# First stage of a two-layer attention and expert network: the product of the normalised rows with the attended rows is made by GpSimd instead of VectorE

## The reference, cut to what matters

```
c = layernorm(x)
s = (c @ w_c + b_c) + (q @ w_q + b_q) + einsum(c, q, w_cq) + b_cq
a = softmax(s, over q)          c2q = a @ q
b = softmax(max(s), over c)     q2c = b @ c      (one row for each sequence)
z = concat([c, c2q, c * c2q, c * q2c]) @ W_l.T + b_l
x = x + z
```

## Time and profile before

| what | value |
|---|---|
| time, median of 3 runs | 1287.81 us (1287.68 to 1289.49) |
| span of the profiled execution | 1303.4 us |
| TensorE busy in the span | 1239.4 us (95%) |
| VectorE busy | 998.1 us (77%) |
| ScalarE busy | 813.5 us (62%) |
| GpSimd busy | 512.1 us (39%) |
| mean granted TensorE clock | 0.982 of full speed |

### The profile page before, as it was taken

How to read it: one execution, slowest core, us unless ns; L and a number is a source line. 1 busy time by engine, 2 the same in 40 slices (tenths; PEclk the granted TensorE clock), 3 DMA queues, 4 the chain that set the end, 5 groups by cost and what they waited for, 6 DMA issues and landing times.

```text
span 1303.4 us, 44045 instructions
## 1 busy us (share of the span) xinstructions
PE 1239.4 (95%) x17244; PEld 1117.8 (86%) x17245; DVE 998.1 (77%) x2454; ACT 813.5 (62%) x1552; POOL 512.1 (39%) x553
## 2 busy tenths in 40 slices
PE   6899999984999999998899999999999999999997
PEld 5788888874999999996688888888888888888886
DVE  4888888875555555536988898889888988898884
ACT  4477766642655555565567666766676667666753
POOL 2466666654121212135544344424442444343010
PEclk9899999997899999998899999999999999999999
DMA  3124333112422222213101110111011101110000
GB/s 110 64 80 147 96 122 82 64 68 71 134 82 72 80 72 80 73 53 76 33 16 34 35 33 16 34 34 29 21 35 34 33 16 34 34 33 12 11 11 18
DMA packets 86536, 71.21 MB, mean 55 GB/s; under 512 B 25088, under 2 KB 73216, under 8 KB 86368
## 3 DMA queue, kind: packets, MB, share of 16 engines
q1 hardware_dynamic: 74768, 42.71, 11.4%
q0 software_dynamic: 11600, 26.10, 6.5%
HBM read 40.73 MB, written 28.05 MB: 53 GB/s over the span
## 4 chain that ended last, share of the span: by engine, by line
PE 83%; DVE 10%; issue 3%; POOL 1%; ACT 1%; DMA 1%; another core or an unknown queue 0%; SPq 0%; DVEq 0%; POOLq 0%; ACTq 0%
PE c_ps_w L84 23%; PE d_ps_y L1218 10%; PE c_ps_w L1731 8%; PE d_ps_h L84 8%; PE c_ps_s L1697 5%; PE c_ps_w L1720 4%; PE c_ps_w L1706 4%; PE c_ps_w L1748 4%; PE a_ps_w L84 3%; PE a_ps_w L917 2%; PE a_ps_w L872 2%; PE a_ps_w L825 1%; PE d_ps_x L1197 1%; PE c_ps_w L1603 1%; DVE a_a_diag L670 1%
## 5 line engine op out<-in xcount | busy, mean ns | idle before, releaser
L1484 POOL DMA_INDIRECT c_back<-sorted_y,k_y_row_of x112 | 112.8, 1007 | 177.8 <-PE c_ps_w L1720 144.8
L93 POOL DMA_INDIRECT sorted_x<-a_xn,f_slot_of x128 | 127.9, 999 | 84.5 <-PE a_ps_w L917 36.6
L1218 PE MATMUL d_ps_y<-e_w_all,d_h_t 128*128 x1136 | 139.1, 276 | 0.0
L1083 POOL DMA_DIRECT2D sorted_y<-d_y_rows x71 | 50.8, 716 | 213.0 <-DVE d_y_rows L1114 208.8
L1218 PEld LDWEIGHTS d_ps_y<-e_w_all,d_h_t 128*128 128x128 f32 x1136 | 134.0, 193 | 0.0
L1731 PEld LDWEIGHTS c_ps_w<-c_wo,c_o_t 128*128 128x128 f32 x1024 | 122.5, 192 | 5.6 <-ACT c_o_t L1945 1.4
L1731 PE MATMUL c_ps_w<-c_wo,c_o_t 128*128 128x128 f32 x1024 | 124.9, 275 | 0.9 <-ACT c_o_t L1945 0.6
L1945 ACT COPY c_o_t<-c_ps_w 128x512 f32<-128x512 f32 x128 | 68.8, 590 | 78.4 <-PE c_ps_w L1720 78.4
L1510 POOL TENSOR_TENSOR c_rstd<-c_var,c_minus_half 128x1 f32<-128x1 f32 x64 | 35.7, 558 | 200.0 <-DVE c_var L2135 200.0
L1166 ACT ACTIVATE d_h_t<-d_ps_h,d_biases 128x256 f32<-128x256 f32 x284 | 111.7, 475 | 2.5 <-PE d_ps_h L84 2.1
L2152 DVE TENSOR_TENSOR c_shifted<-c_ps_s,c_mask 128x1024 f32<-128x1024 f32 x64 | 78.0, 1219 | 41.7 <-PE c_ps_s L1697 41.6
(11 more groups left out here) (264 smaller groups left out, 3596.1 us busy)
## 6 DMA issues: line engine op xcount, KB each, us to landing
d_x_rows<-sorted_x SPq DMA_DIRECT2D x71, 128.0 KB, 2.1
sorted_y<-d_y_rows POOLq DMA_DIRECT2D x71, 128.0 KB, 2.2
k_X<-in_x SPq DMA_DIRECT2D x16, 256.0 KB
a_q_rows<-in_ctx SPq DMA_DIRECT2D x16, 256.0 KB
ctx_cols<-a_q_t SPq DMA_DIRECT2D x16, 256.0 KB
k_ctx_raw<-ctx_cols SPq DMA_DIRECT2D x16, 256.0 KB, 3.9
out<-k_X SPq DMA_DIRECT2D x15, 256.0 KB, 3.1
sorted_x<-a_xn,f_slot_of POOLq DMA_INDIRECT x128
```

The costliest lines, as they stand in the source:

```text
L93: pool.indirect_dma_start(out=sorted_x, out_offset=bass.IndirectOffsetOnAxis(ap=slot_of[:, choice, t:t + 1], axis=0), in_=xn2[:, k, :], in ...
L1218: last = pe.matmul(ps_y[c % 2][:, k * D:(k + 1) * D], h_t[c % 2][:, j, k * P:(k + 1) * P], w2_all[:, ds(e * HC + j, 1), :].rearrange("p a ...
L1484: pool.indirect_dma_start(out=back[:, choice, k, :], out_offset=None, in_=sorted_y, in_offset=bass.IndirectOffsetOnAxis(ap=y_row_of[:, cho ...
```

## The change

GpSimd gets a new step, `cross`, as the last of its turn, behind `root1`: it waits until `z` of the group before has been made (the last reader of `cc_t`) and until `c2q_t` of its own group is complete, and then makes the same product of the same two buffers into the same third. VectorE's instruction for it is taken out. The semaphore that `make_z` waits for is the same and is now raised by GpSimd. Nothing else is changed.

```diff
@@ gpsimd
+            def cross(g):
+
+                if g >= 1:
+                    pool.wait_ge(full, full_at("z", g - 1))
+                pool.wait_ge(c2q_ready, NB * (g + 1))
+                pool.tensor_tensor(cc_t[:], c2q_t[:], c_t[g % 2][:], ALU.mult).then_inc(cc_ready, 1)
+
@@ gpsimd, the end of a turn
                 if t + 2 < G:
                     root1(t + 2)
+                if a is not None:
+                    cross(a)
@@ vector, weighted(g)
-                dve.tensor_tensor(cc_t[:], c2q_t[:], c_t[g % 2][:], ALU.mult).then_inc(cc_ready, 1)
```

## The result

The changed kernel takes 1306.29 us (median of 4 runs, 1301.10 to 1307.24); the kernel before took 1288.65 beside it (4 runs). The ratio is 1.0128, 95 % interval [1.0113, 1.0142]: 17.6 us slower. The forecast was 1294.1, with 1298.7 as its upper end: the direction was right, the size too small by more than half.

What follows compares the result with a forecast made beforehand. VectorE's list between L648 and L842 was taken to set the steady turn. 0 for L716, 5.6 for held ranks and 0.7 for the last group, 6.3 in all, added to 1287.81 gave 1294.1 us; range 1288.4 to 1298.7.

Steps and rivals of the forecast that it cites:

- the slack at L648: At the scores' maxima in turns 3 to 14, VectorE waits 0.625 us a turn, which absorbs part of each delay.
- The hold: At L562 and L563, the product begins as L562 ends and holds L563 about 1.09 us; 0.465 a turn remains.
- the price from the earlier trace: At L2176 in the third stage, a GpSimd product cost VectorE's second two-operand instruction about 1.09 us.
- The last group: In turn 16, `z` starts about 0.7 us later behind the product; bounds 0 to 3.0, the upper if TensorE's clock falls.
- L716 is worth nothing: Removing VectorE's product, 0.73 us a turn, gains 0, since the wait for `gate` at L550 grows to 1.34.
- the twelve turns: Products of turns 2 to 13 meet the ranks of turns 3 to 14: 12 x 0.465 = 5.6 us, bounds 0 to 7.9.
- the delay of the first scatters: On GpSimd, the first scatter issues some 1.6 us later, the second about 1; the delay is gone by the third.
- the clock stays up in steady turns: At TensorE in the 12 turns; the rival, a clock falling every turn, gave 34 us, 1322, chance 0.04.
- GpSimd is the one that waits: Rival at the ranks: the product waits until L566, turns cost nothing, the last group 0.7; 1288.5 us, chance 0.15.
- VectorE's relief counts: Rival: the end of VectorE's turn sets the pace, 16 x 0.73 = 11.7 us go, 1276.1 us, chance 0.05.

Runs made afterwards that it cites:

- the second of before: The kernel before, unchanged, profiled once more: 1289.01 us, ratio 0.9995, profile span 1287.8 where the first profile had 1303.4.
- the run with one comparison more: The kernel before with a first rank comparison made twice on VectorE, ahead of L562 in each turn: 1294.99 us, ratio 1.0053.
- the fill: The kernel before, with GpSimd filling a 128 by 1280 tile with zeros at the place of the change: 1288.49 us, ratio 1.0003.
- the half product: The changed kernel with GpSimd making only the first 256 of 512 columns, VectorE the others where L716 was: 1293.57 us, ratio 1.0043.
- idle, 1.03 us: The kernel before, with GpSimd also multiplying a constant tile by itself at the place of the change, result unread: 1299.23 us, ratio 1.0079.
- full, later: The changed kernel with the product of groups 2 to 14 put behind the second scatter of the next turn: 1308.40 us, ratio 1.0153.
- full, earlier: The changed kernel with the product right behind `root2` in the same turn, `root1` behind it, ahead of the last two scatters: 1307.62 us, ratio 1.0150.
- the last kernel: GpSimd's product waits for VectorE's four normalised rows, ahead of its last scatter; VectorE writes 128 by 8 unread zeros where L716 stood: 1288.69 us, ratio 0.9994.

## Why the prediction was right in direction and too small

The first stage is where nearly all of it is lost: the spans of the two profiles, after and the second of before, are 17.7 us apart, and the experts' first matmuls, at 326.1 and 309.6, already 16.5. By the starts of `gate` that is 10.9 in eleven turns, 2.24 in the turn after them, 2.5 in the last group, and 0.9 in the rest.

**The step that failed: the slack at L648.** The prediction took 0.625 off each hold, from the earlier trace rows, and wrote that "the first stage's turns are the same work in both", the profiled execution and the runs. They were the same work but not the same time: that execution had turns of 17.1 where the usual one has 16.73, and in it VectorE had a wait at L648 that the second profile doesn't have and the run with one comparison more rules out for the runs. The 15.6 us between its span and the median was a sign, and it was put aside, though 4.35 of it is all that lies in these turns. What the runs have is 0.2 at L575, behind L648, where the prediction saw nothing idle. With it a turn loses 1.20 - 0.2 = 1.00 instead of 0.465: 12 turns cost 12 us and not 5.6. Of the difference, 12 x 0.425 = 5.1 is the slack and 12 x 0.11 = 1.3 the longer hold. What held L648 back in that one execution stays open: the records of the scores stand where they stand in the other.

**The hold: nearly the right size, in the wrong order.** 1.20 us instead of 1.09, and on the first comparison rather than the second. The prediction had the product wait for the end of L562 and become 1.5 to 1.6 long; it didn't wait, and was 1.26. The sentence on the Trainium skill (SBUF — State Buffer, Who interferes with whom) gave all of the product, 1.28; the measured 1.20 of 1.26 lies by it, so the page was nearer than the price from the earlier trace rows. The same section says that a GpSimd instruction that only writes is no contender, and that a VectorE operation with one tensor and scalars can take the shared ports in a fast mode. The comparison beside the fill (0.42) and the normalisation (1.30 us) agree with both. How the price goes with length and place:

| product | held on VectorE | lost us | turn longer by |
|---|---|---|---|
| half, 0.72 to 0.94 us | second comparison | 0.53 | 0.30 |
| idle, 1.03 us | first comparison | 0.97 | 0.75 |
| full, 1.26 us | first comparison | 1.20 | 1.00 |
| full, later | sum of the counts | 1.50 | 1.22 |
| full, earlier | a row normalisation | 0.96 | 0.90 |

The first four stand ahead of L575 and get 0.2 to 0.3 back there; the last stands behind it and gets 0.06.

**The last group: near its upper bound in one profile.** Forecast 0.7, with 3.0 if the clock should fall. The late start is 0.84, so the 0.7 was nearly right. In the profile after the clock fell as well, and the cost is 2.5; in that of the product later it stayed up beside the same idle times, and the cost is 0.86. Whether it fell in the other timed runs of the changed kernel no run shows.

**A term that was missing.** 1.25 us in one turn, by the batch weights that GpSimd's offset overtook, as in the earlier trace rows. The prediction counted only the instructions that move.

**Right:** L716 is worth nothing (the wait for `gate` took all of it); the twelve turns, by number (turns 15 and 16, which the prediction ruled out, are held by 0.3, but turn 15 is 16.62 long in both profiles); the delay of the first scatters is free (the fill shows it); the clock stays up in steady turns, granted 1.00, with `z` at 3.81.

**The rivals.** "GpSimd is the one that waits" didn't happen; the half product shows that it can for a part. "VectorE's relief counts" fell: with every hold taken away, in the last kernel, the time is that of the kernel before.

## What to carry to other kernels

Before slack is taken from a profile, compare its span with the median of the runs, and profile once more where they differ: the execution that was 15.6 us too long also showed 0.6 us of slack in each turn that the runs didn't have. A product moved to GpSimd can cost about its own length (1.50 us at most here, with a product of 1.28) on the VectorE instruction that then reads two operands from SBUF, even one of 0.17 us, or normalises a row; put it where VectorE waits or reads a PSUM bank, and make it wait for that place. And if VectorE waits for another engine at the end of its list anyway, taking work off it gains nothing: the best version here ends where the kernel before stood.

## What the runs showed of the hardware that was not expected

- A VectorE instruction is held though it starts ahead of GpSimd's record: the comparison by 0.07 to 0.17 us, the sum of the counts by 0.36. So the recorded starts don't tell which of the two goes first. The Trainium skill (Perfetto Trace Analysis, GPSIMD Engine Instruction) says that such an instruction starts on the cores before the profiler's start, and that its spans are not to be relied on; the rows agree. From when on GpSimd holds VectorE up, no run here shows.
- A row normalisation with one tensor operand and two scalars of a row is held like a two-operand instruction (1.30 us instead of 0.34). Two products that read one operand from a PSUM bank are not: 0.73 us for both, beside GpSimd's product of 1.27 and without it.
- The choice by rank, with one tensor operand, lasted 0.42 us beside the fill's later scatters and 0.34 with one comparison more, instead of 0.20, and ended with a scatter of GpSimd. That the scatter holds it was not tested by a run of its own.
- One instruction less in each turn of VectorE's list made one instruction, in one turn, start 0.24 us late; it then lost its place to GpSimd and 1.0 us more. All five kernels whose list was shorter in the middle groups have it, in the same turn, and all five have the product on GpSimd; the seven profiles in which an instruction stands there (two of the kernel before) don't. A write of 65 ns put in its place takes it away. What in the list's position does this stays open.
